# Graph attention on one Trainium2 core: 12 of 784 row gathers replaced by copies of single rows issued from SyncE

## Chip, cores and metric

The kernel runs on one core of a Trainium2 chip. The metric is the device time of one execution in microseconds (us), the median of several runs. The engines are named as the profile names them: PE (TensorE), DVE (VectorE), ACT (ScalarE), POOL (GpSimd), SP (SyncE). "SPq" or "DVEq" is an engine's instruction queue: DMA issues, waits, register work.

## What is computed

Two graph layers follow each other over N = 6250 nodes and E = 100,000 edges sorted by target. Cut to what matters (the change lies in the second layer alone):

```python
h = jnp.maximum(_layernorm(x), 0.0)
x = x + gnn_layer0(h, edge_index, edge_attr)      # edge MLP, sum over edges, node MLP 256-1024-1024-256
h = jnp.maximum(_layernorm(x), 0.0)
# layer 1: attention with K = 8 heads of 32 features
h_prime = (h @ W + b).reshape(n, 8, 32)
h_src, h_trg = jnp.sum(h_prime * a_src, 2), jnp.sum(h_prime * a_trg, 2)
e = leaky_relu(h_src[src] + h_trg[trg])
exp_e = jnp.exp(e - jnp.max(e))
alpha = exp_e / (segment_sum(exp_e, trg)[trg] + 1e-10)
x = x + segment_sum(h_prime[src] * alpha[:, :, None], trg).reshape(n, 256)
```

`src` and `trg` hold the edges and a loop at every node.

## The kernel before

The program has five stages: `prepare` (norms, tables), `edges0` (edge stage of the first layer), `nodes` (its node stage, which also writes the table `tab1` of 6250 rows of 264 float32 numbers: 256 features and 8 source scores), `edges1` (the attention over edges) and `finish` (division and output).

`edges1` takes the edges in NB = 196 batches of 512. A batch is CB = 4 chunks of 128 edges, one edge to a partition. Four batches (RING) are a round; there are 49. For each batch:

- **POOL** gathers the 128 source rows of each chunk from `tab1` into `rows` (named `a_rows` in the profile), one indirect DMA for a chunk (L1458), 784 in all. `rows` has DEEP = 8 slots, one batch each. From the ninth batch on POOL waits on `rows_free` before it fills a slot again (L1455).
- **SP** waits until the four gathers of the batch have landed (L1437) and passes that on with `rows_in` (L1438). Only this tells DVE that the batch is in. Behind it SP issues the batch's other loads, in program order: in the second and fourth batch of a round the target numbers of two batches to come, broadcast to all partitions (`dstb`, L1417, behind a wait for `dstb_free`); in the second also one tile of each node's own row (`hs`, L1431), behind a wait for `hs_free`, which DVE gives when it has added the tile before (`add_self`, L1627); in the third two loads of the first layer's result (`acc` and `x_tail`, L1427 and L1428).
- **PE** turns the target scores to the edges with one-hot matrices (`ht_ps`, L1511), and later sums weighted rows into node tiles (`sum_ps`, L1524).
- **DVE** adds source and target scores (`e`, L1609, which needs `rows_in`), weights the rows (`feat`, L1616), makes the one-hot matrices (L1593, L1632), adds sums to `acc` (L1621). Once a round it reads the next tile bounds, 16 whole numbers, from SBUF into registers (`spans_of`, L1308).
- **ACT** takes the exponentials (`feat` and `p_ps`, L1468 and L1469) and scales the nodes' own rows (L1474). Its loop body is one round.

All engines run the batches in program order. Every queue is in order: what stands behind a wait waits too. The queue of SP is written out for all 196 batches, without a loop.

```python
for b in range(NB):
    i, u = divmod(b, RING)
    sp.wait_ge(rows_ready[b % DEEP], 16 * CB * (b // DEEP + 1))
    sp.sem_inc(rows_in, 1)
    ...
```

Of the kernel before, what the change touches and what calls it, by code (L numbers as in the profile page):

```python
# [1 line left out]

# [3 lines left out]
F32, F16, I32, I16 = mybir.dt.float32, mybir.dt.float16, mybir.dt.int32, mybir.dt.int16  # L26
BF16 = mybir.dt.bfloat16
ALU = mybir.AluOpType
ACT = mybir.ActivationFunctionType
# [3 lines left out]
P = 128  # L33
N, D, E, ED, H = 6250, 256, 100000, 64, 1024
TN = 125
NT = N // TN
CB = 4
BE = CB * P
RING = 4
NB = -(-E // (BE * RING)) * RING  # L40
NBP = NB + RING
NCH = NBP * CB
KH, KD = H // P, D // P
HEADS, HD = 8, 32
TW = D + HEADS
# [5 lines left out]
PG = 5  # L51
WROWS = KD + KH + KH * D // H
FAR = -1.0e30
CAP = 87.0


def build(nc, t, out):

    with ExitStack() as ctx:
# [18 lines left out]
        with ExitStack() as first:  # L78
# [5 lines left out]
            with ExitStack() as edge_mlp:  # L84
# [3 lines left out]
                edges0(nc, t, dram, sb)  # L88
            nodes(nc, t, dram, sb, stale)
        maxima, selfmax, ctrg, x1_tail = edges1(nc, t, dram, sb, keep)  # L90
        finish(nc, t, dram, sb, maxima, selfmax, ctrg, x1_tail, out)

# [1222 lines left out]
def edges1(nc, t, dram, sb, keep):  # L1315
# [8 lines left out]
    with ExitStack() as ctx:  # L1324
        m = Memory(nc, ctx)
# [5 lines left out]
        DEEP = 2 * RING  # L1331
# [11 lines left out]
        rows = m.sb("a_rows", [P, DEEP, CB, TW], F32)  # L1343
# [5 lines left out]
        part = m.sb("part", [TN, HEADS], F32)  # L1349
        smax_col = m.sb("smax_col", [HEADS, 1], F32)  # L1350
        diag = m.sb("diag", [HEADS, HEADS], F32)
        ones = m.sb("a_ones", [HEADS, P], F32)
        tiny = m.sb("a_tiny", [1, 1], F32)
        spare = m.sb("a_spare", [1, 1], F32)

# [13 lines left out]
        rows_ready = [m.sem(f"a_rows_ready{s}") for s in range(DEEP)]  # L1369
# [10 lines left out]
        xhot_ready = m.sem("a_xhot_ready")  # L1380
        xsum_done = m.sem("a_xsum_done")
        max_read = m.sem("max_read")
        lines = m.sem("a_lines")
        chain_sem = m.sem("a_chain")
        LAST = NB // RING - 1

        def rounds(eng, body):

            for u in range(RING):
                body(0, u)  # L1390
            with eng.Fori(1, LAST) as i:
                for u in range(RING):
                    body(i, u)
            for u in range(RING):
                body(LAST, u)

        def has(i, u, ahead):
            return not isinstance(i, int) or 0 <= RING * i + u + ahead < NB

        def await_(eng, sem, i, u, k=0, n=1):  # L1400

            if isinstance(i, int):
                eng.wait_ge(sem, 1)
                eng.sem_inc(sem, -1)  # L1404
            else:
                eng.wait_ge(sem, n * u + k + 1)
                if (u, k) == (RING - 1, n - 1):
                    eng.sem_inc(sem, -n * RING)
# [3 lines left out]
        @block.sync  # L1412
        def _(sp):
            dst_rows = t["dst_flat"].rearrange("(b r e) -> b (r e)", r=PAIR, e=BE)

            def load(pair, h):
                sp.dma_start(dstb[:, h * PAIR:(h + 1) * PAIR, :].rearrange("p r e -> p (r e)"),  # L1417
                             dst_rows[bass.ds(pair, 1)].broadcast_to([P, PAIR * BE])).then_inc(dstb_ready[h], 16)

            load(0, 0)  # L1420
            sp.dma_start(table[:, 0:NBP + 1, :], dram["spans"][0:NBP + 1, :].unsqueeze(0)).then_inc(ld_tab, 16)
            load(1, 1)
            x1_v, fits = dram["x1"].rearrange("(t p) c -> p t c", p=TN), 2 * D - TW
            tab_v = dram["tab1"].rearrange("(t p) c -> p t c", p=TN)

            def load_x1(tiles):
                sp.dma_start(acc[0:TN, tiles, TW:2 * D], x1_v[:, tiles, 0:fits]).then_inc(ld_x1, 16)  # L1427
                sp.dma_start(x1_tail[:, tiles, :], x1_v[:, tiles, fits:D]).then_inc(ld_x1, 16)  # L1428

            def load_self(tile):  # L1430
                sp.dma_start(hs[:], tab_v[:, bass.ds(tile, 1), 0:D].rearrange("p a c -> p (a c)")).then_inc(hs_ready, 16)  # L1431

            load_self(NT - 1)
            load_x1(slice(LAST + 1, NT))
            for b in range(NB):
                i, u = divmod(b, RING)
                sp.wait_ge(rows_ready[b % DEEP], 16 * CB * (b // DEEP + 1))  # L1437
                sp.sem_inc(rows_in, 1)  # L1438
                if i < LAST and u % PAIR == 1:
                    sp.wait_ge(dstb_free, b // PAIR + 1)  # L1440
                    load(2 * (i + 1) + u // PAIR, u // PAIR)
                if u == 1:
                    sp.wait_ge(hs_free, i + 1)
                    load_self(i)
                if u == 2:
                    load_x1(slice(i, i + 1))
            sp.wait_ge(ld_x1, 32 * (LAST + 2))

        @block.gpsimd
        def _(pool):  # L1450
            for b in range(NB):
                if b == 1:
                    pool.dma_start(dsts[:], t["dst_cols"]).then_inc(ld_dst, 16)
                if b >= DEEP:
                    pool.wait_ge(rows_free, b - DEEP + 1)  # L1455
                for k in range(CB):
                    c = CB * b + k
                    pool.indirect_dma_start(  # L1458
                        rows[:, b % DEEP, k, :], None, dram["tab1"],
                        bass.IndirectOffsetOnAxis(ap=srcs[:, c:c + 1], axis=0),  # L1460
                    ).then_inc(rows_ready[b % DEEP], 16)

        @block.scalar
        def _(act):
            act.activation(tiny[:], sb["lneps"][0:1, :], ACT.Exp)

            def exponents(s, row):
                act.activation(feat[:, row, :, D:TW], d[:, s], ACT.Exp)  # L1468
                act.activation(p_ps[:], d[:, s], ACT.Exp).then_inc(p_ready, 1)  # L1469

            def scaled(tile, heads):
                for h in heads:
                    f = slice(h * HD, (h + 1) * HD)
                    ins = act.activation(hs[:, f], hs[:, f], ACT.Copy,  # L1474
                                         scale=pself[:, bass.ds(tile, 1), h:h + 1].rearrange("p a c -> p (a c)"))
                if HEADS - 1 in heads:
                    ins.then_inc(hs_scaled, 1)

            def loaded():
                act.wait_ge(hs_ready, 16)  # L1480
                act.sem_inc(hs_ready, -16)

            act.wait_ge(self_in, 1)
            act.sem_inc(self_in, -1)
            act.activation(pself[:], eself[:], ACT.Exp).then_inc(self_exp, 1)
            act.wait_ge(d_ready, 1)
            act.sem_inc(d_ready, -1)
            exponents(0, 0)
            act.wait_ge(self_exp, 1)
            loaded()  # L1490
            scaled(NT - 1, range(HEADS))

            def body(i, u):
                s = u % 2
                if has(i, u, 1):
                    await_(act, d_ready, i, u)
                    exponents(1 - s, (u + 1) % RING)
                if u:
                    if u == 1:
                        loaded()  # L1500
                    scaled(i, range(HEADS)[3 * (u - 1):3 * u])

            rounds(act, body)

        @block.tensor
        def _(pe):
# [76 lines left out]
        def _(dve):  # L1583
            def settled(ins):
                ins.then_inc(chain_sem, 1)
                dve.wait_ge(chain_sem, 1)
                dve.sem_inc(chain_sem, -1)
# [58 lines left out]
            dve.memset(ones[:], 1.0)  # L1646
            dve.memset(maxima[:], FAR)
            dve.tensor_copy(iota_ps[:], iota16[:])
            dve.memset(nid[96:KT, :], float(N))
            settled(dve.memset(trg[0:KT], 0.0))  # L1650
            dve.tensor_copy(nid[0:TN, :], nodeid[0:TN, :])
            settled(dve.memset(trg[96:KT, 0, :, 0:HEADS], FAR))
            dve.wait_ge(smax_turned, 1)
# [128 lines left out]
def finish(nc, t, dram, sb, maxima, selfmax, ctrg, x1_tail, out):  # L1782

    with ExitStack() as ctx:  # L1784
# [57 lines left out]
        def _(dve):  # L1842
            def settled(ins):
                ins.then_inc(chain_sem, 1)
                dve.wait_ge(chain_sem, 1)
                dve.sem_inc(chain_sem, -1)
# [11 lines left out]
            settled(dve.tensor_scalar(c[:], ctrg[:], top[0:TN, :], -1.0, ALU.subtract, ALU.mult))  # L1858
            settled(dve.tensor_scalar(c[:], c[:], CAP, None, ALU.min))
            dve.sem_inc(exp_in, 1)  # L1860
# [54 lines left out]
```

## Time and profile before

| | |
|---|---|
| three runs | 3154.38, 3159.45, 3160.02 us; median 3159.45 us |
| profiled execution, from its first to its last instruction (span) | 3157.3 us; no time of its own is listed beside it |
| busy of the span | PE 2446.9 (77%), DVE 2156.6 (68%), POOL 1976.9 (63%), ACT 1488.6 (47%) |
| attention stage, first gather to last | 2114.6 to 3103.3 us |
| gathers of the stage | 784, mean 957 ns |
| DMA queues, share of 16 engines over the whole span | POOL's 23.5%, SP's 17.4% |

The program is a sequence of stages with different limits, so the shares over the whole span say little about the stage that is changed. The rows of the stage itself stand in a section below. Busy time leaves out waits, register work and DMA issues of a queue. What ended an idle time is inferred from semaphore events.

### The profile page before, as it was taken

The page shows a single profiled execution, that of the slowest core. Times are in us where ns is not written, and L with a number is a line of the kernel's source. Part 1 is how long each engine was busy: PE and PEld are TensorE (multiplying, and loading weights), DVE is VectorE, ACT ScalarE, POOL GpSimd, SP SyncE. Part 2 cuts the span into 40 slices and gives each one's busy share as a digit, 9 for nine tenths or more (in the row PEclk, how much of TensorE's full clock was granted, in tenths as well). Part 3 has the DMA queues.
Part 4 walks back from the last instruction along what each step waited for, and adds up shares of the span by engine and source line. Part 5 has one row for each costly group of instructions (what it writes and reads, how often), then busy time and mean ns, then how long its engine had stood idle before and what let it go on. Part 6 is the DMA issues. An engine that isn't in the chain of part 4 may idle for free. (4 is left out here: it accounts for less than half of the span.)

```text
span 3157.3 us, 79016 instructions
## 1 busy us (share of the span) xinstructions
PE 2446.9 (77%) x25310; PEld 2164.9 (69%) x25311; DVE 2156.6 (68%) x3833; ACT 1488.6 (47%) x3803; POOL 1976.9 (63%) x2143
## 2 busy tenths in 40 slices
PE   0577777777777789999999999947777777777763
PEld 0466666666666679999999999945555555555552
DVE  7676667777677636666666666657766766666666
ACT  5444444444444458888888888831111111111114
POOL 4677777777777634444444444437777777777772
PEclk9998889999899889999999999978888888887996
DMA  6555555555555500000000000026555655555554
GB/s 158 168 161 149 158 154 166 161 163 160 159 164 158 143 25 18 21 21 20 20 21 20 20 22 21 21 61 178 171 173 173 174 172 168 173 172 173 171 170 136
DMA packets 183839, 373.69 MB, mean 118 GB/s; under 512 B 42598, under 2 KB 93688, under 8 KB 183769
## 3 DMA queue, kind: packets, MB, share of 16 engines
q0 software_dynamic: 75552, 209.66, 23.5%
q1 hardware_dynamic: 107392, 162.37, 17.4%
q10 hardware_dynamic: 824, 0.87, 0.1%
q8 instruction: 27, 0.44, 0.1%
q14 instruction: 44, 0.35, 0.0%
HBM read 346.95 MB, written 25.80 MB: 118 GB/s over the span
## 5 line engine op out<-in xcount | busy, mean ns | idle before, releaser
L446 POOL DMA_INDIRECT rows<-tab_scratch,srcs x784 | 765.7, 977 | 238.7 <-issue 234.1
L1458 POOL DMA_INDIRECT a_rows<-tab_scratch,srcs x784 | 750.5, 957 | 251.7 <-issue 235.8
L1524 PE MATMUL sum_ps<-feat,a_hot 128*125 128x264 f32 x1960 | 601.5, 463 | 237.5 <-DVE feat L1616 121.0
L1524 PEld LDWEIGHTS sum_ps<-feat,a_hot 128*125 128x125 f32 x1960 | 417.4, 222 | 341.7 <-DVE feat L1616 133.9
L876 PE MATMUL z_ps<-ah,w 128*128 128x125 f16 x6400 | 553.8, 219 | 1.0 <-PEq L982 1.0
L876 PE MATMUL z_ps<-al,w 128*128 128x125 f16 x3200 | 542.7, 217 | 0.0
L876 PEld LDWEIGHTS z_ps<-ah,w 128*128 128x128 f16 x6400 | 489.5, 97 | 1.5 <-issue 1.4
L1468 ACT ACTIVATE feat<-d 128x32 f32<-128x32 f32 x196 | 44.9, 229 | 827.0 <-DVE d L1612 566.2
L500 PE MATMUL mlp_ps<-ewa,eab 128*128 128x256 f16 x788 | 203.5, 290 | 284.3 <-PEq L496 283.3
L478 ACT ACTIVATE rh<-mlp_ps 128x1024 f16<-128x1024 f32 x196 | 199.7, 1019 | 358.2 <-ACTq L477 347.7
L829 POOL TENSOR_TENSOR a<-a 128x500 f32<-128x500 f32 x100 | 124.4, 1244 | 372.1 <-POOLq L828 372.1
L507 PE MATMUL sum_ps<-rows,hot 128*125 128x256 f16 x980 | 296.4, 302 | 76.8 <-DMA rows<-tab_scratch,srcs 55.8
L1059 ACT ACTIVATE a<-z,pack 128x125 f32<-128x125 f32 x800 | 321.4, 484 | 11.9 <-ACTq L1055 7.8
L876 PEld LDWEIGHTS z_ps<-al,w 128*128 128x128 f16 x3200 | 315.2, 98 | 0.8
L500 PEld LDWEIGHTS mlp_ps<-ewa,eab 128*128 128x128 f16 x788 | 81.9, 104 | 327.4 <-issue 315.1
L509 PE MATMUL sum_ps<-rh,hot 128*125 128x256 f16 x980 | 291.2, 297 | 0.0
L508 PE MATMUL sum_ps<-rows,hot 128*125 128x256 f16 x980 | 291.1, 297 | 0.0
L510 PE MATMUL sum_ps<-rl,hot 128*125 128x256 f16 x980 | 289.9, 296 | 0.0
L579 DVE SCALAR_TENSOR_TENSOR rl<-mlp_ps,rh 128x1024 f16<-128x1024 f32 x196 | 240.0, 1225 | 34.3 <-DVEq L578 29.2
L1031 ACT ACTIVATE z<-z_ps,pack 128x125 f32<-128x125 f32 x800 | 226.3, 371 | 37.5 <-ACTq L1029 37.5
L1616 DVE TENSOR_TENSOR feat<-a_rows,p_ps 128x1024 f32<-128x1024 f32 x196 | 239.1, 1220 | 3.9 <-DVEq L1404 0.5
L507 PEld LDWEIGHTS sum_ps<-rows,hot 128*125 128x125 f16 x980 | 148.3, 151 | 116.9 <-DMA rows<-tab_scratch,srcs 71.0
(211 smaller groups left out, 5422.8 us busy)
## 6 DMA issues: line engine op xcount, KB each, us to landing
ea<-edge_t SPq DMA_DIRECT2D x394, 128.0 KB
dstb<-dst_flat SPq DMA_DIRECT2D x98, 512.0 KB
rows<-tab_scratch,srcs POOLq DMA_INDIRECT x784
a_rows<-tab_scratch,srcs POOLq DMA_INDIRECT x784
tab_scratch<-prow SPq DMA_DIRECT2D x50, 128.9 KB
hx<-x SPq DMA_DIRECT2D x50, 125.0 KB
x_scratch<-x SPq DMA_DIRECT2D x50, 125.0 KB
hs<-tab_scratch SPq DMA_DIRECT2D x50, 125.0 KB
```

The costliest lines, as they stand in the source:

```text
L446: pool.indirect_dma_start(rows[:, b % DEEP, k, :], None, dram["tab0"], bass.IndirectOffsetOnAxis(ap=srcs[:, c:c + 1], axis=0),).then_inc(r ...
L500: pe.matmul(mlp_ps[:, s, k, :], eab[:, s, e], ewa[:], start=True, stop=False)
L507: pe.matmul(out[:, 0:D], lhs, rows[:, ring, k, 0:D], start=(k == 0), stop=False, skip_group_check=True)
L508: pe.matmul(out[:, 0:D], lhs, rows[:, ring, k, D:2 * D], start=False, stop=False, skip_group_check=True)
L509: pe.matmul(out[:, D:2 * D], lhs, rh[:, s, k, :], start=False, stop=False, skip_group_check=True)
L510: ins = pe.matmul(out[:, D:2 * D], lhs, rl[:, s, k, :], start=False, stop=(k == CB - 1), skip_group_check=True)
L579: dve.scalar_tensor_tensor(out=rl[:, s].rearrange("p k d -> p (k d)"), in0=mlp_ps[:, s].rearrange("p k d -> p (k d)"), scalar=0.0, in1=rh[ ...
L876: ins = pe.matmul(out, lhs, rhs, start=(k == 0 and q == 0), stop=(k == n - 1 and q == 2))
L1059: ins = act.activation(a[j][:, k, :], z[j][:, k, :], ACT.Relu, bias=cols[be][:, k:k + 1], scale=cols[g][:, k:k + 1])
L1458: pool.indirect_dma_start(rows[:, b % DEEP, k, :], None, dram["tab1"], bass.IndirectOffsetOnAxis(ap=srcs[:, c:c + 1], axis=0),).then_inc(r ...
L1524: ins = pe.matmul(out[:], hot[:, h, k, :], feat[:, row, k, :], start=(k == 0), stop=(k == CB - 1))
L1616: return dve.tensor_tensor(feat[:, u, :, 0:D].rearrange("p k (h f) -> p k h f", h=HEADS), slot_of(slot)[:, :, 0:D].rearrange("p k (h f) -> ...
```

## The change

SP loads single rows. Every 16th batch from number 19 on (19, 35, ..., 195: 12 batches, `SINGLES`) POOL gathers three chunks, not four. The 128 rows of the fourth are fetched by 128 DMAs of one row each (1056 bytes), issued by SP, eight behind each of the 16 batches b = 0..15, 16..31 and so on up to 191. Each such piece (`load_side`) first reads eight row numbers from SBUF into registers, then issues eight DMAs whose DRAM address is worked out from a register. They land in `side`, two buffers of 128 rows. ACT copies `side` into the batch's slot of `rows` (`single`), three batches ahead of its use, and counts `side_kept`; SP waits for it before it passes that batch on. The row numbers come from a new input `src_rows` through 12 small loads at the stage's start, on which SP waits before the first batch. ACT's loop is written out over eight rounds.

```diff
--- before.py
+++ after.py
@@ -51,6 +31,9 @@
 PG = 5
 WROWS = KD + KH + KH * D // H
 FAR = -1.0e30
+EVERY = 4 * RING
+AHEAD = EVERY + RING - 1
+SINGLES = [b for b in range(AHEAD, NB, EVERY)]
 CAP = 87.0
 
 
@@ -1350,6 +1333,8 @@
         smax_col = m.sb("smax_col", [HEADS, 1], F32)
         diag = m.sb("diag", [HEADS, HEADS], F32)
         ones = m.sb("a_ones", [HEADS, P], F32)
+        side = m.sb("side", [P, 2, TW], F32)
+        side_src = m.sb("side_src", [len(SINGLES), P], I32)
         tiny = m.sb("a_tiny", [1, 1], F32)
         spare = m.sb("a_spare", [1, 1], F32)
 
@@ -1380,6 +1365,9 @@
         xhot_ready = m.sem("a_xhot_ready")
         xsum_done = m.sem("a_xsum_done")
         max_read = m.sem("max_read")
+        ld_side = m.sem("ld_side")
+        side_in = [m.sem(f"side_in{q}") for q in range(2)]
+        side_kept = m.sem("side_kept")
         lines = m.sem("a_lines")
         chain_sem = m.sem("a_chain")
         LAST = NB // RING - 1
@@ -1430,11 +1418,25 @@
             def load_self(tile):
                 sp.dma_start(hs[:], tab_v[:, bass.ds(tile, 1), 0:D].rearrange("p a c -> p (a c)")).then_inc(hs_ready, 16)
 
+            def load_side(m_, first, n):
+
+                _, at = nc.values_load_multi_w_load_instructions(
+                    side_src[m_:m_ + 1, first:first + n], engines=[mybir.EngineType.SP], min_val=0, max_val=N - 1,
+                    skip_runtime_bounds_check_because="src names nodes: 0 to N - 1")
+                for j in range(n):
+                    sp.dma_start(side[first + j:first + j + 1, m_ % 2, :], dram["tab1"][bass.ds(at[j], 1), :]).then_inc(side_in[m_ % 2], 16)
+
             load_self(NT - 1)
             load_x1(slice(LAST + 1, NT))
+            for m_, b in enumerate(SINGLES):
+                sp.dma_start(side_src[m_:m_ + 1, :], t["src_rows"][CB * b + CB - 1:CB * b + CB, :]).then_inc(ld_side, 16)
+            sp.wait_ge(ld_side, 16 * len(SINGLES))
             for b in range(NB):
                 i, u = divmod(b, RING)
-                sp.wait_ge(rows_ready[b % DEEP], 16 * CB * (b // DEEP + 1))
+                fewer = len([x for x in SINGLES if x <= b and x % DEEP == b % DEEP])
+                sp.wait_ge(rows_ready[b % DEEP], 16 * (CB * (b // DEEP + 1) - fewer))
+                if b in SINGLES:
+                    sp.wait_ge(side_kept, SINGLES.index(b) + 1)
                 sp.sem_inc(rows_in, 1)
                 if i < LAST and u % PAIR == 1:
                     sp.wait_ge(dstb_free, b // PAIR + 1)
@@ -1444,6 +1446,11 @@
                     load_self(i)
                 if u == 2:
                     load_x1(slice(i, i + 1))
+                m_, part = divmod(b, EVERY)
+                if m_ < len(SINGLES):
+                    if part == 0 and m_ >= 2:
+                        sp.wait_ge(side_kept, m_ - 1)
+                    load_side(m_, part * P // EVERY, P // EVERY)
             sp.wait_ge(ld_x1, 32 * (LAST + 2))
 
         @block.gpsimd
@@ -1453,7 +1460,7 @@
                     pool.dma_start(dsts[:], t["dst_cols"]).then_inc(ld_dst, 16)
                 if b >= DEEP:
                     pool.wait_ge(rows_free, b - DEEP + 1)
-                for k in range(CB):
+                for k in range(CB - (b in SINGLES)):
                     c = CB * b + k
                     pool.indirect_dma_start(
                         rows[:, b % DEEP, k, :], None, dram["tab1"],
@@ -1500,7 +1507,28 @@
                         loaded()
                     scaled(i, range(HEADS)[3 * (u - 1):3 * u])
 
-            rounds(act, body)
+            def single(i, q):
+
+
+                act.wait_ge(side_in[q], 16 * P)
+                act.sem_inc(side_in[q], -16 * P)
+                act.activation(rows[:, AHEAD % DEEP, CB - 1, :], side[:, q, :], ACT.Copy).then_inc(side_kept, 1)
+
+            def kept(i, q=None):
+                for u in range(RING):
+                    body(i, u)
+                    if u == 0 and q is not None:
+                        single(i, q)
+
+            kept(0)
+            with act.Fori(0, len(SINGLES) // 2 - 1) as n:
+                for q in range(2):
+                    for r in range(1, 5):
+                        kept(8 * n + 4 * q + r, q if r == 4 else None)
+            first = 8 * (len(SINGLES) // 2 - 1) + 1
+            assert len(SINGLES) % 2 == 0 and first + 7 == LAST
+            for i in range(first, LAST + 1):
+                kept(i, (i // 4 - 1) % 2 if i % 4 == 0 else None)
 
         @block.tensor
         def _(pe):
@@ -1902,6 +1930,7 @@
     dst = np.concatenate([np.asarray(inputs["dst"]), np.full(pad, N, np.int32)])
     a["src_cols"] = np.ascontiguousarray(src.reshape(NCH, P).T)
     a["dst_cols"] = np.ascontiguousarray(np.concatenate([np.full(BE, N, np.int32), dst]).reshape(NCH + CB, P).T)
+    a["src_rows"] = np.ascontiguousarray(src.reshape(NCH, P))
     a["dst_flat"] = dst
     ea = np.concatenate([np.asarray(inputs["edge_attr_64"]), np.zeros((pad, ED), np.float32)])
     a["edge_t"] = np.ascontiguousarray(ea.reshape(NBP, BE, ED).transpose(0, 2, 1))
```

In SP's queue, the first batches of the stage. Before (the words in brackets are semaphores waited for ahead of the instruction):

```order
L1417 DMA dstb<-dst_flat 128x1024 [waits a_rows_ready0,a_rows_ready1,dstb_free]
L1431 DMA hs<-tab_scratch 125x256 [waits hs_free]
L1427 DMA acc<-x_scratch 125x248 [waits a_rows_ready2]
L1428 DMA x_tail<-x_scratch 125x8
L1417 DMA dstb<-dst_flat 128x1024 [waits a_rows_ready3,dstb_free]
```

and now the second batch, with eight pairs of register work (ISA) and DMA in each batch, of which one stands here (the lines of the kernel have moved; L1405 is the load of `dstb`, L1419 that of `hs`, L1415 that of `acc`, L1423 the read of eight row numbers):

```order
L1405 DMA dstb<-dst_flat 128x1024 [waits a_rows_ready1,dstb_free]
L1419 DMA hs<-tab_scratch 125x256 [waits hs_free]
L1423 TENSOR_LOAD side_src
L1427 ISA
L1427 DMA side<-tab_scratch 1x264
```

The eight row copies of the second batch stand behind its `hs` load. Then, for the third batch:

```order
L1415 DMA acc<-x_scratch 125x248 [waits a_rows_ready2]
L1416 DMA x_tail<-x_scratch 125x8
L1423 TENSOR_LOAD side_src
L1427 ISA
L1427 DMA side<-tab_scratch 1x264
```

The wait for the third batch's gathers (`a_rows_ready2`) now stands behind the register read and the eight row copies of the second batch, and with them behind its wait for `hs_free`.

## Rows read from the trace of the kernel before

**Rows 1.** Busy time by engine, 48 rounds of the attention stage (2137.7 to 3098.5 us)

```profile
core 0: us, PE busy (x) PEld busy (x) DVE busy (x) ACT busy (x) POOL busy (x), PEclk, DMA share, GB/s
2137.70:3098.50 960.80, 718.62 (x5199) 544.78 (x5200) 670.71 (x1588) 146.99 (x768) 728.62 (x763) 0.86 0.59 172
```

**Rows 2.** Timeline of POOL: start us, us, instruction, idle before it

```profile
2499.42 0.95 POOL L1458 DMA_INDIRECT a_rows<-tab_scratch,srcs  x1 [0.30 <-issue]
2500.68 0.94 POOL L1458 DMA_INDIRECT a_rows<-tab_scratch,srcs  x1 [0.31 <-issue]
```

**Rows 3.** Waits of POOL in the stage: us in total, times, longest us

```profile
POOL a_rows L1458 <- issue: 235.8, 774, 0.3
...
POOL a_rows L1458 <- DVE a_hot L1632: 2.7, 9, 0.3
```

**Rows 4.** Waits of SP's queue, the same 48 rounds

```profile
SPq L1438 <- DMA a_rows<-tab_scratch,srcs: 739.7, 189, 5.6
SPq L1431 <- DVE acc L1627: 130.3, 49, 7.5
```

**Rows 5.** Waits of DVE, the same 48 rounds

```profile
DVE e L1609 <- SPq L1438: 105.7, 84, 2.7
DVE e L1609 <- DVEq L1705: 88.0, 44, 3.3
DVE e L1609 <- PE a_used_ps L1537: 43.9, 24, 2.2
```

**Rows 6.** Timeline of SP's DMA issues: stage start, then one round's third batch

```profile
2114.33 0.26 SPq L1421 DMA_DIRECT2D table<-spans_scratch  x1
2114.64 0.36 SPq L1417 DMA_DIRECT2D dstb<-dst_flat  x1
...
2516.19 0.28 SPq L1427 DMA_DIRECT2D acc<-x_scratch  x1
2516.51 0.34 SPq L1428 DMA_DIRECT2D x_tail<-x_scratch  x1
```

**Rows 7.** SP, line L800 in node stage: ns min/median/max, first and last start

```profile
L800 SPq DMA_DIRECT2D x_scratch<-x x50: 262/263/290, 1180.6 to 2102.4; - x50
L800 SPq MOVE x_scratch<-x x44: 29/29/29, 1199.0 to 2017.6; - x44
```

**Rows 8.** SP, line L796 (its DRAM source address comes from a register)

```profile
L796 SPq DMA_DIRECT2D hx<-x x50: 267/285/302, 1109.5 to 2081.2; - x50
L796 SPq FUSED_REGOPS  x44: 46/56/65, 1181.1 to 2006.1; - x44
```

**Rows 9.** Timeline of SP in the first edge stage, two issues with a MOVE between

```profile
501.28 0.47 SPq L410 DMA_DIRECT2D ea<-edge_t  x1
501.84 0.56 SPq L411 DMA_DIRECT2D ea<-edge_t  x1
```

**Rows 10.** Register reads: L336, first edge stage; L1308, attention stage (16 values)

```profile
L336 DVEq TENSOR_LOAD <-st x101: 308/812/849, 95.1 to 1100.4; - x101
L336 PEldq TENSOR_LOAD <-st x66: 1003/1467/1665, 101.1 to 1083.2; - x66
...
L1308 DVEq TENSOR_LOAD <-table x51: 542/1105/1429, 2119.1 to 3113.8; - x51
L1308 PEldq TENSOR_LOAD <-table x51: 551/1107/1467, 2128.7 to 3112.9; - x51
```

**Rows 11.** Timeline, DVE and SP, second batch of one round

```profile
2509.87 0.35 SPq L1417 DMA_DIRECT2D dstb<-dst_flat  x1
...
2510.64 0.19 DVE L1609 TENSOR_TENSOR e<-a_rows,ht_ps 128x32 f32<-128x32 f32 x1 [1.67 <-SPq L1438]
2510.79 1.22 DVE L1616 TENSOR_TENSOR feat<-a_rows,p_ps 128x1024 f32<-128x1024 f32 x1
...
2511.93 0.42 DVE L1627 TENSOR_TENSOR acc<-acc,hs 125x256 f32 x1
...
2512.37 0.28 SPq L1431 DMA_DIRECT2D hs<-tab_scratch  x1
```

**Rows 12.** SP's relays to DVE (L1438)

```profile
L1438 SPq EVENT_SEMAPHORE  x196: 17/17/17, 2123.6 to 3107.7; - x196
```

**Rows 13.** ACT, the nearest copy-like operation in shape (node stage)

```profile
L1103 ACT ACTIVATE hx<-hx,nmr,rstd x50: 585/624/625, 1162.4 to 2090.8; 125x256 f32<-125x256 f32 x50
```

**Rows 14.** DMA queues, the same 48 rounds: packets, MB, share of 16 engines

```profile
q0 software_dynamic: 36562, 102.99, 38.3%
q1 hardware_dynamic: 32400, 62.10, 20.8%
```

## The prediction

> **What bounds the kernel now.** The change touches the attention stage alone, so I read that stage and leave the shares over the whole span aside. First the busy time of its 48 full rounds [rows 1], taken from one issue of `hs` to the 48th after it: 960.8 us, or 20.02 us for a round of four batches. POOL is busy 728.62 us, PE about as long. The timeline of POOL tells them apart: gather follows gather, 0.95 us each with 0.30 us between [rows 2], and the waits of POOL say that this gap is "issue" 774 times and a wait for a free slot only 9 times, 2.7 us together [rows 3]. POOL never stops, so POOL sets the pace: four times 1.25 us is 5.0 us for a batch. DVE and PE follow. DVE waited 105.7 us for SP's word that a batch is in [rows 5], so it has room, and the eight slots let POOL run on when DVE lags for some batches.
>
> Then SP, where the change puts its work. In these 48 rounds SP waited 739.7 us for gathers to land, 15.41 us a round, and 130.3 us in 49 waits for `hs_free`, 2.66 us each [rows 4]. What is left of 20.02 us, 1.95 us, is its own work: five DMA issues and the relays. SP has room of 15.4 us a round. But it is the relay between the gathers and DVE, and its queue is in order.
>
> **What is taken away.** 12 gathers of 0.95 + 0.30 us: 15.1 us, all of it on the path as long as POOL sets the pace. A round would then take 20.02 - 15.1/49 = 19.7 us on average.
>
> **What is added to SP.** For 192 of the 196 batches one register read of eight numbers and eight DMAs with an address from a register. I call their sum S.
>
> *One DMA.* A single-row issue is seen once in this stage, the load of `table`, 0.26 us, and the next issue starts 0.31 us after it [rows 6]. An issue whose DRAM target comes from a register took the same (263 ns in the middle, [rows 7]), one whose DRAM source does 285 ns at 125 rows [rows 8]. I take 0.265 and a gap of 0.05. Ahead of it stands the register work: 0.046 us in its shortest case [rows 8] and a MOVE of 0.029 us [rows 7]. The order of the new queue shows the first but not the second; the trace has a MOVE before each such issue in the loops, so I count it. Each of the two brings a gap: between two issues with one MOVE between them pass 0.56 - 0.47 = 0.09 us, so a gap is 0.03 us [rows 9]. Together 0.046 + 0.029 + 0.06 + 0.265 + 0.05 = 0.45 us, eight times 3.6 us.
>
> *The register read.* SP has none in this trace. The rows of other queues bound it: 16 numbers took 1.105 us on DVE in this stage, and two numbers 0.542 us (the shortest there, at the stage's end) [rows 10]. In the first edge stage six took 0.812 us on DVE and 1.467 us on PE [rows 10]. Eight numbers lie between 0.54 us and PE's line carried on: from four (1.003) to six (1.467) 0.23 us a number, so 1.93 us for eight. Interpolating in the rows of this stage gives 0.78 us, carrying on DVE's line from one number (308 ns) to six 1.01 us. I take their middle, 0.9 us, and 0.03 us of gap.
>
> So S = 3.6 + 0.93 = 4.53 us.
>
> **The sum.** Four S are 18.1 us, and SP had 15.4 us to spare. SP becomes the bound. The chain of a round then runs through SP, with one stretch through DVE: in its second batch SP relays, issues `dstb`, and waits for `hs_free`, which comes only after DVE has done `e`, `feat` and the addition to `acc`. From DVE's `e` to the issue of `hs` pass 1.73 us [rows 11], from the relay at least 0.2 us more, of which 0.4 us lie beside the issue of `dstb`. So the wait cannot fall below 1.5 us, and above it stands the 2.66 us of today [rows 4]. DVE's own register read falls just before this batch (its 88.0 us behind L1705, 2.0 us each, [rows 5]) and holds it back, so I take 2.0 us. The round is then 4 x 4.53 + 1.95 + 2.0 = 22.07 us against 20.02 us. Over 48 rounds that is 98 us. The last four batches have no row copies and need not wait for POOL: 2 us back. The saved gathers give nothing, because POOL then stops for free slots. Forecast: +96 us, a span of 3157.3 + 96 = 3253.3 us. The median of the runs is 2.15 us above that span, so 3255.5 us for the median.
>
> **What lies beside other work.** ACT's copy of 128 x 264 numbers: the nearest row, 125 x 256 with scale and bias, took 0.62 us [rows 13]; 12 of them are 7.5 us on an engine busy for 147 of 960.8 us [rows 1], and it stands behind the exponentials, so nobody waits for it. If the rows have not landed by then, ACT holds back the next exponentials; see the third rival. The 12 small loads of row numbers: 12 x 0.31 = 3.7 us of issue from about 2116 us, and their landing; the first relay came at 2123.6 us [rows 12], so they are hidden or cost a microsecond once, ahead of DVE's first use of a batch at 2132 us. DMA traffic: the bytes are the same. The gathers hold 38.3% of the 16 engines and SP's loads 20.8% [rows 14]. Should all single rows fall on one engine, its share of gather work would grow by 8 rows on 32 per batch, a quarter of 38%: still under 70%, no bound.
>
> **Rivals.**
>
> *SP keeps up, and it gets faster.* If S is at most (19.7 - 3.95) / 4 = 3.94 us, POOL stays the pace-maker and the 15.1 us are won: 3144 us. This is the mechanism on the other side, and its deciding point is only 0.6 us below my S. It needs the register read near its floor, 0.54 us, or no MOVE before the issues (8 x 0.06 = 0.48 us less), and better both. For it speaks that the new queue's order shows no MOVE; against it that the trace shows it with each issue of this kind. Chance 0.12. Just above that point, up to S of about 4.05 us, the two effects cancel: within 0.2% (about 6 us, what a measurement of this kernel can tell from no change), chance 0.04.
>
> *The register read costs what PE paid.* 1.93 us makes S = 5.56 us and a round 26.2 us: +297 us, 3456 us. For it speaks only that both PE rows of the first edge stage lie on that line; against it that in the attention stage PE read 16 numbers in 1.107 us [rows 10]. Chance 0.06.
>
> [...]
>
> *ACT waits for the rows.* The last eight are issued behind the relay of the batch two before the copy's place, and behind a `dstb` of 512 KB in SP's queue. If they land late by 5 us, DVE gets the next exponentials late 12 times: up to 60 us on top, 3315 us. Against it: with SP as the bound two relays, 9 us, pass in between. Chance 0.08.
>
> **How the numbers follow.** The forecast's own case (SP is the bound, S from 4.05 to about 5.2 us) has 0.70. Its ends: S = 4.05 gives a round of 20.15 us and +6 us, S = 5.2 gives 24.75 us and +227 us. Faster 0.12, same 0.04, slower 0.84. The range leaves out the faster and the level case and the PE-like read above 3400 us, with a little of the forecast's low end: 3170 to 3400 us. The likeliest is 3255 us.
>
> **What the changed profile would show.** Right: POOL's waits for a free slot grow from 2.7 us to about a hundred; SP's waits for gathers fall from 15.4 us a round to nearly nothing; DVE waits for L1438's successor some 3 us a round longer; pieces of eight issues at 0.45 us pitch; rounds of 22 us. Wrong: POOL's gathers still in steps of 1.25 us without a stop, or the register read on SP under 0.4 us, or issues at a pitch of 0.3 us, or above 0.6 us.

## The result, and the profile after

| | before | changed |
|---|---|---|
| median of the runs | 3159.45 us | 3247.29 us |
| lowest, highest | 3154.38, 3160.02 us | 3245.29, 3250.71 us |
| span of the profiled execution (its time) | 3157.3 us | 3248.9 us (3250.71 us) |

The changed kernel takes 1.0284 times as long, with a 95% interval of 1.0270 to 1.0299: 88 us slower. 96 us had been forecast.

The busy times of the 48 rounds of the attention stage, again from one issue of `hs` to the 48th after it (to be held against [rows 1]):

```profile
core 0: us, PE busy (x) PEld busy (x) DVE busy (x) ACT busy (x) POOL busy (x), PEclk, DMA share, GB/s
2141.50:3192.10 1050.60, 763.59 (x5198) 577.10 (x5198) 667.79 (x1587) 150.77 (x779) 724.37 (x755) 0.80 0.54 158
```

These rounds took 1050.6 us, not 960.8 us: 21.89 us a round, not 20.02. That is 89.8 us of the 91.6 us between the two spans; the way from the last issue of `hs` to the end became 2 us shorter (58.8 to 56.8 us), and the first gather began 3.8 us later, which is a difference of the stages ahead. DVE and ACT did the same work in both. PE's part grew, at a mean granted clock of 0.80 in place of 0.86.

The waits of POOL in the whole stage (against [rows 3]), then, in the 48 rounds, those of SP's queue (against [rows 4]) and DVE's (against [rows 5]); the columns are us in total, times, the longest:

```profile
POOL a_rows L1465 <- issue: 209.1, 686, 0.3
POOL a_rows L1465 <- DVE a_hot L1660: 100.4, 85, 3.5
```

```profile
SPq L1419 <- DVE acc L1655: 147.7, 48, 7.5
```

```profile
DVE e L1637 <- SPq L1440: 184.7, 82, 3.5
DVE e L1637 <- DVEq L1733: 67.1, 44, 2.2
DVE e L1637 <- PE a_used_ps L1565: 63.8, 38, 2.4
```

POOL now stops for free slots, 100 us of it. SP's wait for gathers, 739.7 us before, has no row any more: each batch has landed when SP comes to it. The one wait that SP has left is that for DVE's addition, and it grew from 2.66 to 3.08 us a round. DVE's waits for SP's word grew by 79 us, 1.6 us a round.

What SP does in its queue (ns min/median/max; against [rows 7, 8, 10]), and ACT's copy (against [rows 13]):

```profile
L1427 SPq FUSED_REGOPS  x1536: 37/37/43, 2129.9 to 3184.5; - x192
L1427 SPq MOVE side<-tab_scratch x1536: 29/29/29, 2130.0 to 3184.6; - x192
L1427 SPq DMA_DIRECT2D side<-tab_scratch x1536: 224/228/283, 2130.0 to 3184.7; - x192
...
L1423 SPq TENSOR_LOAD <-side_src x192: 696/779/952, 2129.1 to 3180.8; - x192
...
L1515 ACT ACTIVATE a_rows<-side x12: 406/407/407, 2227.9 to 3193.1; 128x264 f32<-128x264 f32 x12
```

One round in the timeline of SP's DMA issues (start us, length us; issues of the same kind in a row are merged, with the gaps and register reads between them):

```profile
2574.93 0.37 SPq L1405 DMA_DIRECT2D dstb<-dst_flat  x1
2576.22 7.30 SPq L1427 DMA_DIRECT2D side<-tab_scratch  x16
2583.63 0.37 SPq L1405 DMA_DIRECT2D dstb<-dst_flat  x1
2586.88 0.27 SPq L1419 DMA_DIRECT2D hs<-tab_scratch  x1
2588.14 3.16 SPq L1427 DMA_DIRECT2D side<-tab_scratch  x8
2591.42 0.27 SPq L1415 DMA_DIRECT2D acc<-x_scratch  x1
2591.74 0.34 SPq L1416 DMA_DIRECT2D x_tail<-x_scratch  x1
2593.07 3.52 SPq L1427 DMA_DIRECT2D side<-tab_scratch  x8
2596.71 0.37 SPq L1405 DMA_DIRECT2D dstb<-dst_flat  x1
```

From one last-batch `dstb` (2574.93) to the next (2596.71) the queue is full but for one hole, 2584.00 to 2586.88: the wait for `hs_free`. Sixteen issues with one register read and a relay between them take 7.30 us, so two batches are 7.30 + 0.78 + gaps, and a piece with its read is S = 0.78 + 0.03 + 8 x 0.41 = 4.1 us.

The same moment in DVE's timeline (the columns as there):

```profile
2580.08 0.19 DVE L1637 TENSOR_TENSOR e<-a_rows,ht_ps 128x32 f32<-128x32 f32 x1 [1.13 <-DVEq L1733]
...
2585.14 0.19 DVE L1637 TENSOR_TENSOR e<-a_rows,ht_ps 128x32 f32<-128x32 f32 x1 [1.99 <-issue]
2585.29 1.22 DVE L1644 TENSOR_TENSOR feat<-a_rows,p_ps 128x1024 f32<-128x1024 f32 x1
2586.43 0.42 DVE L1655 TENSOR_TENSOR acc<-acc,hs 125x256 f32 x1
```

SP had passed the second batch on just before 2583.63. DVE began it only at 2585.14, 5.06 us after it had begun the first, so SP did not set this stretch of the chain. DVE works until 2583.15, reads its 16 tile bounds (1.1 us from 2583.50) and then needs PE's scores for the second batch. The `DVEq L1733` ahead of the first batch's `e` is not this read: it is a step of 21 ns by which DVE counts a semaphore (`max_read`) down. This is the point at which the prediction's sum was put together wrongly; it comes back below.

### The profile page after: what moved, and what is told of

Read it like the earlier page. It is cut to its first block and busy times, and to the rows that moved or that the text cites. A ratio compares the mean times of both kernels' runs of the same rounds, so it can differ in the third digit from the quotient of the medians.

```text
span 3248.9 us, 83679 instructions
## 1 busy us (share of the span) xinstructions
PE 2493.2 (77%) x25310; PEld 2197.4 (68%) x25311; DVE 2154.1 (66%) x3833; ACT 1492.4 (46%) x3815; POOL 1968.2 (61%) x2131
## 5 line engine op out<-in xcount | busy, mean ns | idle before, releaser
L1465 POOL DMA_INDIRECT a_rows<-tab_scratch,srcs x772 | 741.7, 961 | 322.7 <-issue 209.1
L1552 PE MATMUL sum_ps<-feat,a_hot 128*125 128x264 f32 x1960 | 652.7, 493 | 284.9 <-DVE feat L1644 203.3
L1552 PEld LDWEIGHTS sum_ps<-feat,a_hot 128*125 128x125 f32 x1960 | 446.8, 238 | 402.5 <-DVE feat L1644 220.4
L1637 DVE TENSOR_TENSOR e<-a_rows,ht_ps 128x32 f32<-128x32 f32 x196 | 36.8, 188 | 351.5 <-SPq L1440 184.7
```

Source lines behind the costliest of these rows:

```text
L1465: pool.indirect_dma_start(rows[:, b % DEEP, k, :], None, dram["tab1"], bass.IndirectOffsetOnAxis(ap=srcs[:, c:c + 1], axis=0),).then_inc(r ...
L1552: ins = pe.matmul(out[:], hot[:, h, k, :], feat[:, row, k, :], start=(k == 0), stop=(k == CB - 1))
```

## The experiments

Each kernel is the changed one with one edit; where fewer DMAs fill `side`, the count that ACT waits for follows. Its time is held against runs of the kernel before on the same chip, with a 95% interval for the ratio. The kernel before took 3158.5 to 3163.28 us on the chips of these runs, so two versions are compared by their ratios (1.0284 for the changed kernel); one hundredth of the ratio is 31.6 us.

### Rows first, then the wait

```diff
-                if u == 1:
-                    sp.wait_ge(hs_free, i + 1)
-                    load_self(i)
-                if u == 2: ...
                 m_, part = divmod(b, EVERY)
                 ...
                     load_side(m_, part * P // EVERY, P // EVERY)
+                if u == 1:
+                    sp.wait_ge(hs_free, i + 1)
+                    load_self(i)
+                if u == 2: ...
```

> The eight row copies of a round's second batch stand ahead of the wait for hs_free and of the load of hs, not behind them. Theory (SP's queue is the bound, because its own 4 x 4.13 us of copies and 2.3 us of other issues stand in one line with the 3.1 us wait for DVE): the wait then runs out beside the copies, a round on SP falls to 18.8 us, below POOL's 19.7 us, POOL sets the pace again and the 12 saved gathers count: about 3144 us (3140 to 3155). Rival (the traffic of 1536 single-row DMAs slows the loads or the gathers): nothing changes, 3247 us. Rival (ACT's copy or its wait for the rows holds up the exponentials): nothing changes, 3247 us.

Measured: 3155.75 us against 3163.28 us, ratio 0.9973 (0.9963 to 0.9983). The 88 us are gone, and the kernel is 0.3% faster than the one before. All 1536 row copies, all of ACT's work and the same DMA traffic are still there, so neither rival can hold. SP's waits in the 48 rounds, and POOL's in the stage, which again takes gather after gather:

```profile
SPq L1440 <- DMA a_rows<-tab_scratch,srcs: 56.4, 65, 3.7
SPq L1419 <- DVE acc L1655: 6.8, 2, 3.4
```

```profile
POOL a_rows L1465 <- issue: 234.3, 769, 0.3
...
POOL a_rows L1465 <- DVE a_hot L1660: 0.6, 2, 0.3
```

The wait for DVE has shrunk to 6.8 us, and SP has 56.4 us of slack again, 1.2 us a round. Only 7.5 of the 15 us expected were won in the median; the profiled run, at 3147.34 us, was the fastest of ten (the highest 3158.64 us). Why the others took longer is not settled: with 1.2 us of slack a round small delays can come through, but no profile shows them.

### All gathers back on POOL

```diff
-                for k in range(CB - (b in SINGLES)):
+                for k in range(CB):
...
-                act.activation(rows[:, AHEAD % DEEP, CB - 1, :], side[:, q, :], ACT.Copy).then_inc(side_kept, 1)
+                act.sem_inc(side_kept, 1)
```

> All 784 gathers are back on POOL; SP still issues the 1536 row copies, ACT only counts them and no longer copies them (that copy is left out). Theory: POOL had stopped for free slots, so 12 gathers more cost nothing: 3247 us (3240 to 3254), with POOL's waits for slots some 15 us shorter. Rival (the saving is already inside the 3247 us): 15 us more, 3262 us. Rival (ACT's copy and its chain cost time): clearly below 3247 us.

Measured: 3247.89 us, ratio 1.0271 (1.0254 to 1.0288), the same as the changed kernel. Twelve gathers more and twelve copies on ACT fewer change nothing. POOL's waits for slots took up the gathers, 100.4 us before, now

```profile
POOL a_rows L1464 <- DVE a_hot L1659: 82.7, 78, 1.9
```

So in the changed kernel the saving was worth nothing. Gathers and ACT's copies were changed together here, so the time alone could hide two effects that cancel. The 17.7 us by which POOL's waits shrank cover the 15.1 us of twelve gathers, and no instruction is seen to wait for ACT's copy in the changed kernel's trace; that ACT's part cost nothing rests on that.

### The same traffic in one DMA a batch

```diff
-                _, at = nc.values_load_multi_w_load_instructions(...)
-                for j in range(n):
-                    sp.dma_start(side[first + j:first + j + 1, m_ % 2, :], dram["tab1"][bass.ds(at[j], 1), :])...
+                at = (m_ * P + first) * 4
+                sp.dma_start(side[first:first + n, m_ % 2, :], dram["tab1"][at:at + n, :])...
```

> The eight single-row DMAs of a batch and their register read are replaced by one DMA of eight neighbouring rows at a fixed address: the same bytes and rows of traffic, other rows than the edges name, so that part of the computation is changed. Theory: SP loses only about 0.3 us a batch, POOL sets the pace: 3144 us (3140 to 3152). Rival (traffic): stays near 3247 us.

Measured: 3148.52 us, ratio 0.9955 (0.9939 to 0.9972). The rows still travel, only the number of issues has fallen to one a batch. The rows are others than the edges name. This is what the twelve gathers are worth when SP has room: 14.8 us by the median ratio (9 to 19 us by its interval), where 15.1 us had been worked out.

```profile
SPq L1437 <- DMA a_rows<-tab_scratch,srcs: 652.7, 188, 5.3
SPq L1419 <- DVE acc L1652: 140.3, 49, 7.5
```

SP's slack is back at 13.6 us a round. The wait for DVE is there too, 2.9 us a round, and does no harm.

### Seven rows of eight

```diff
-                for j in range(n):
+                for j in range(7):
...
+            for q in range(2):
+                sp.dma_start(side[:, q, :], dram["tab1"][0:P, :]).then_inc(ld_side, 16)
```

> SP issues seven of the eight row copies of each batch; the sixteen rows of a chunk that are left out keep what was loaded once at the start, so that part of the computation is changed. Theory: each copy is 0.41 us of the bound, 4 x 0.41 x 48 = 79 us for all rounds: 3168 us (3158 to 3178), a round of 20.2 us. Rival (a fixed cost per batch, the register read or the relay behind it): 3235 us or more. Rival (DMA traffic in proportion): an eighth of the 103 us between 3144 and 3247 us, so about 3234 us.

Measured: 3193.56 us, ratio 1.0094 (1.0077 to 1.0111). The two rivals fall, but so does the number: 0.0190 of the ratio, or 60 us (54 us by the medians), were won, not 79. SP's wait for `hs_free` shows where the rest went:

```profile
SPq L1419 <- DVE acc L1657: 174.1, 49, 7.1
```

It has grown from 3.08 to 3.55 us a round. When SP's piece behind the first batch gets shorter, SP is only earlier at a wait that DVE ends, and waits longer. Three pieces of a round are on the chain, not four: 3 x 0.41 x 48 = 59 us. Each trace shows the same over 45 rounds (the 3rd to the 47th, means worked out from the starts of SP's relays and issues):

| | from the first batch's relay to the second's | from the first batch's relay to the issue of `hs` |
|---|---|---|
| before | 4.6 us | 7.6 us |
| changed | 4.2 us | 7.7 us |
| seven rows of eight | 3.8 us | 7.8 us |
| six rows of eight (next run) | 3.4 us | 8.0 us |
| shifted by 4 bytes (below) | 5.4 us | 7.7 us |

The way to the issue of `hs` hardly moves, though in the changed kernels the first stretch of it goes from 3.4 to 5.4 us.

### Six rows of eight

The same edit with 6.

> SP issues six of the eight row copies of each batch (the other rows keep what was loaded once, so part of the computation is changed). By the three-piece chain a round on SP would be 20.7 - 3 x 0.41 = 19.5 us, just below POOL's 19.7 us: 3150 us (3146 to 3162), a gain of some 40 us on seven rows, where the chain alone would give 59 us. Rival (cost in proportion to copies without a threshold): 3140 us or less.

Measured: 3148.07 us against 3158.5 us, ratio 0.9965 (0.9953 to 0.9978). Going from eight rows to seven won 60 us by the ratios, from seven to six 41 us, and then POOL is the bound again, as expected. SP hardly has slack, 9.6 us in all:

```profile
SPq L1419 <- DVE acc L1657: 201.4, 49, 5.9
SPq L1442 <- DMA a_rows<-tab_scratch,srcs: 9.6, 9, 3.0
```

### Rows spread unevenly: a miss

```diff
-                    load_side(m_, part * P // EVERY, P // EVERY)
+                    sizes = (11, 7, 7, 7)
+                    load_side(m_, part // RING * sum(sizes) + sum(sizes[:u]), sizes[u])
```

> The same 1536 row copies and the same result, but spread 11, 7, 7, 7 over the four batches of a round, not 8, 8, 8, 8. Theory formed on the run with seven rows (54 us won, not the 79 us expected): only three of a round's four pieces of copies lie on the chain; the one behind the first batch lies beside DVE's way from the first to the second batch (its register read and PE's scores, about 5.7 us from SP's relay, with a piece of 4.1 us). Moving three copies there takes 3 x 0.41 us off each round: 59 us, 3188 us (3180 to 3200). Rival (the sum of SP's work counts, all four pieces alike, as in the prediction): no change, 3247 us. Rival (the longer first piece delays the second batch's relay): slower than 3247 us.

Measured: 3344.24 us against 3158.5 us, ratio 1.0580 (1.0562 to 1.0598): 0.0296 of the ratio, 94 us, above the changed kernel. The issues were as long as before. The register read was not:

```profile
L1423 SPq TENSOR_LOAD <-side_src x192: 1329/1712/1776, 2127.1 to 3274.0; - x192
```

Eleven or seven numbers took 1.33 to 1.78 us, where eight had taken 0.70 to 0.95 us. The reads also began at other places: in the changed kernel each starts on a multiple of 32 bytes of its row of the tile, here where the last ended. That puts the eleven on multiples of 128 bytes (1.35 us in the middle) and the sevens 44, 72 and 100 bytes beyond (1.67 to 1.74 us), so count and place changed together. The next three runs take this apart.

### Uneven, but read in line

```diff
-                    side_src[m_:m_ + 1, first:first + n], engines=...
+                    side_src[m_:m_ + 1, 16 * part:16 * part + 8 * -(-n // 8)], engines=...
...
-    a["src_rows"] = np.ascontiguousarray(src.reshape(NCH, P))
+    at = np.concatenate([16 * p + np.arange((11, 7, 7, 7)[p % RING]) for p in range(EVERY)])
+    a["src_rows"] = np.zeros((NCH, 16 * EVERY), np.int32)
+    a["src_rows"][:, at] = src.reshape(NCH, P)
```

> Spread 11, 7, 7, 7 as in the run before it that came out 97 us slower, but SP reads its row numbers 16 or 8 at a time from places that start on a multiple of 64 bytes, not 11 or 7 at a time from wherever the last piece ended. Theory (the loss was the register read, 1.35 to 1.74 us against 0.70 to 0.80 us for eight in line; the three-piece chain holds): reads of 8 take 0.7 to 0.8 us, of 16 some 1.1 us, the first piece is 5.8 us, about as long as DVE's way, and the three others are 0.41 us shorter: 3188 to 3203 us. Rival (the sum of all four pieces counts): 3247 us plus 14 us for the longer read, 3261 us. Rival (the longer first piece itself made the 97 us): above 3300 us.

Measured: 3204.67 us against 3159.61 us, ratio 1.0146 (1.0125 to 1.0166), 2 us above the range. With the same number of row copies and the same result 44 us are won over the even spread, just by where they stand. A sum of all of SP's work would forbid that. The read took what was expected, and the wait for DVE, 82.4 us in all, fell to 1.7 us a round. Three copies off three pieces would be 59 us; the rest went where the first piece now ends: from the first batch's relay to the issue of `hs` pass 8.1 us in the mean, 0.36 us more than in the changed kernel, 17 us over the rounds.

```profile
L1423 SPq TENSOR_LOAD <-side_src x192: 713/794/1222, 2129.7 to 3137.3; - x192
```

```profile
SPq L1419 <- DVE acc L1656: 82.4, 48, 4.4
```

### The row numbers shifted by 4 and by 16 bytes

```diff
-                    side_src[m_:m_ + 1, first:first + n], engines=...
+                    side_src[m_:m_ + 1, 1 + first:1 + first + n], engines=...
```

(4 in place of 1 for 16 bytes; the load of `side_src` is shifted likewise.)

> The changed kernel with its row numbers one column (4 bytes) further on in SBUF; still eight a read, nothing else moved. Theory (a read costs a fifth of a microsecond a number unless it can take eight in line at once): the read takes 1.9 us in place of 0.78 us, three of four lie on the chain, 3 x 1.15 x 48 = 166 us: about 3410 us (3395 to 3440). Rival (it was the odd count, 7 or 11, not the place): the read stays at 0.8 us, 3247 us.

Measured: 3409.91 us against 3159.61 us, ratio 1.0794 (1.0772 to 1.0816).

> As the run before, but shifted by four columns (16 bytes). If 16 bytes in line are enough for the fast read (the read of six on DVE in the first edge stage starts on 16 bytes and took 0.81 us), it stays at 0.8 to 1.0 us and the time at 3247 to 3275 us; if 32 are needed, it is as with 4 bytes, 1.9 us and about 3410 us.

Measured: 3245.88 us, ratio 1.0275 (1.0254 to 1.0295). The reads, first of the one, then of the other:

```profile
L1423 SPq TENSOR_LOAD <-side_src x192: 1842/1923/2100, 2128.4 to 3343.6; - x192
```

```profile
L1423 SPq TENSOR_LOAD <-side_src x192: 698/782/952, 2127.3 to 3179.6; - x192
```

One word of shift makes the same eight numbers cost 1.92 us and not 0.78 us, and costs the kernel 0.0510 of the ratio, 161 us. 3 x 1.14 x 48 = 164 us: the three-piece chain holds in this direction too. A shift by 16 bytes costs nothing that two runs of each could show.

### Two buffers for the nodes' own rows

```diff
-        hs = m.sb("hs", [TN, D], F32)
+        hs = m.sb("hs", [TN, 2, D], F32)
...
-                    sp.wait_ge(hs_free, i + 1)
-                    load_self(i)
+                    if i:
+                        sp.wait_ge(hs_free, i)
+                    load_self(i, (i + 1) % 2)
```

(and a semaphore `hs_ready` for each buffer; ACT and DVE take the buffer of the round's parity.)

> Two buffers for the nodes' own rows, so that SP's wait for hs_free is for the addition of the round before; order of SP's work, row copies and gathers as in the changed kernel. Theory (the pin of SP to DVE once a round turns DVE's way into SP time): the wait vanishes, SP needs 4 x 4.13 + 2.3 = 18.8 us a round, POOL sets the pace at 19.7 us: 3148 us (3143 to 3158). Rival (the sum of SP's own work is too large with or without the wait): above 3200 us. Rival (moving rows first helped for another reason, such as DMA order): stays near 3247 us.

Measured: 3147.32 us against 3158.5 us, ratio 0.9965 (0.9954 to 0.9977). SP's work and its order are as in the changed kernel; only DVE is no longer waited for in the same round. The wait for `hs_free` has no row, and SP has slack:

```profile
SPq L1441 <- DMA a_rows<-tab_scratch,srcs: 45.6, 41, 2.7
```

### Both remedies

> Both remedies together: two buffers for the nodes' own rows and the row copies ahead of their load. Theory: POOL already sets the pace with either, so nothing is added: within 5 us of the two-buffer kernel, 3148 us (3143 to 3156). If a rest of DVE's coupling cost the rows-first kernel some of its 15 us (it won 7.5 us), this one wins it back.

Measured: 3145.2 us against 3158.5 us, ratio 0.9956 (0.9940 to 0.9973). The fastest version with the full result: 13.3 us below the kernel before. Its interval overlaps those of either remedy alone.

## Why the prediction was right, and where it was not

- **What bounds the kernel before, and after.** Right. POOL's pace before and SP's queue after, with POOL held at the free slots (forecast "about a hundred" us, 100.4 us measured). One of the signs was off: DVE was to wait some 3 us a round longer for SP's word, and waited 1.6 us longer.
- **What the gathers are worth.** Right: 15.1 us forecast, 14.8 us (9 to 19) with one DMA a batch, and nothing in the changed kernel, where twelve more gathers left the ratio at 1.0271 against 1.0284.
- **One row copy.** 0.45 us forecast, 0.41 us measured. The MOVE that the order of instructions does not show was there. The issue itself took 228 ns, not 265: the row of `table` [rows 6] was a single issue with none right before it, and the first of each piece here still takes about as long, the others less.
- **The register read.** 0.9 us forecast, 0.78 us measured. Interpolating in the rows of the same stage gave 0.78 us; I had moved off it, to the middle between it and a line through one and six numbers on DVE in the first edge stage. The reads of six numbers on PE there start at odd places (4 bytes beside a multiple of 8), which fits the shifted runs. The rival "costs what PE paid" has its read in the run shifted by 4 bytes: its 1.93 us for eight is 1.92 us there. Its time does not come out, 3410 us and not 3456 us, because one of the four pieces is off the chain. No row stood behind S = 5.2 us as the upper end of the forecast's own case; S was 5.3 us in that run, and its 3410 us lie above the range.
- **S.** 4.53 us forecast, 4.1 us measured (4.15 us in the mean of the 192 pieces): 0.4 us too much, taken four times a round.
- **The chain of a round.** This is the step that failed: "Four S are 18.1 us", with the wait for `hs_free` taken at a fixed 2.0 us. The wait is not fixed. DVE comes to the second batch some 5 us after the first, by its own work and register read and by PE's scores, whatever SP does meanwhile as long as its piece is no longer than that. The 88.0 us behind L1705 [rows 5], which the prediction took for this register read, are waits ahead of the first batch that end in a 21 ns semaphore step; L1705 reads nothing. SP's piece behind the first batch lies beside that, so a round is three S and DVE's way. The seven-row run (60 us, not 79), the uneven one (44 us won with the same work) and the shifted one (161 us) all give three pieces. The wait was 3.08 us where 2.0 had been taken, and 2.66 us was to be its upper bound. It went from 1.7 us (uneven, in line) to 4.1 us (six rows), always against the length of the first piece.
- **Why the sum came out.** Luck, in part. 4 x 0.4 us too much against 1.1 us too little in the wait and 0.3 us in gaps and the other issues: 21.89 us a round measured, 22.07 forecast. The total was good to 8 us because two errors met.
- **The turning point.** Put at S = 3.94 us. Seven rows (S about 3.7 us) were still 1.0094 times the time before, six rows (S about 3.3 us) faster. So it lies between 3.3 and 3.7 us: the forecast had put it too high, because the wait that it held at 2.0 us grows as S shrinks.
- **Beside other work.** ACT's copy took 0.41 us and was waited for by nobody; no wait of ACT for the rows is seen; the same traffic was there in the runs that lost nothing. All as forecast.

## What to carry to other kernels

Idle time of a queue is not room for new work if that queue is in order and relays something: count how much of it lies between which two waits, and put new work where the queue would wait for another engine anyway (here ahead of the wait, not behind it: the same 1536 issues then left a gain of 7.5 us, where 88 us had been lost). A wait that grows when work ahead of it shrinks marks a piece that is off the chain. And before a sum says "four times", ask which of the four lie beside somebody else's way.

## What the hardware showed that I had not expected

- A register read from SBUF depends on where it starts. Eight 4-byte numbers took 0.78 us on SP from places on multiples of 16 or 32 bytes of the tile's row, and 1.92 us from 4 bytes beside. The count matters too: from multiples of 64 bytes or more eleven took 1.33 to 1.51 us, sixteen 1.15 to 1.22 us; seven from 44, 72 or 100 bytes took 1.66 to 1.78 us. Sixteen in line took 1.105 us on DVE [rows 10]; six that start 8 bytes on took 1.429 us there (the longest read of L1308, [rows 10]), against 0.81 us for six from a multiple of 16 bytes. Seven in line were not tried.
- An issue of a one-row DMA took 0.28 us as the first of a piece (the timeline's row below) and 0.228 us behind others of its kind; with the register work for its address eight of them took 3.16 us in the round shown above, a pitch of 0.41 us.

```profile
2142.71 0.28 SPq L1427 DMA_DIRECT2D side<-tab_scratch  x1
```

- Matmuls became slower without any change to them. The 1960 of `sum_ps` took 493 ns in the mean (the row below), 463 ns before, with more holes in PE's work (287 us idle in the 48 rounds, 242 before) and a granted clock of 0.80 on average in the stage, not 0.86 (a mixture of the two levels, 2.4 and 1.2 GHz; single ones took from 385 to 806 ns, 387 ns in the middle, 386 ns before). PE is not busy throughout, but its scores are on DVE's way to the second batch; what the slower matmuls cost in these kernels was not taken apart.

```profile
L1552 PE MATMUL sum_ps<-feat,a_hot 128*125 128x264 f32 x1960 | 652.7, 493 | 284.9 <-DVE feat L1644 203.3
```
